# Attention pooling over 512 behaviour sequences: the fourth group of each chunk split into high and low halves, two of the four relus on ScalarE, a four-column maximum step, and natural tiles loaded two chunks behind the transposed ones

## What is computed

```python
W_b, W_c = (fc1_w[:E], fc1_w[E:])
h = relu(einsum('bse,eh->bsh', behavior_emb, W_b) + (candidate_emb @ W_c)[:, None, :] + fc1_b)
scores = einsum('bsh,h->bs', h, fc2_w[:, 0]) + fc2_b[0]
attn = softmax(scores, axis=-1)
user_interest = einsum('bse,bs->be', behavior_emb, attn)
x = concatenate([user_interest, candidate_emb], axis=1)
z = relu(x @ mlp1_w + mlp1_b)
logit = (z @ mlp2_w + mlp2_b)[:, 0]
```

## Time and profile before

| | |
|---|---|
| median of 3 runs | 282.52 us (282.26 to 283.63) |
| profiled execution, its own time | 283.16 us |
| its span | 281.4 us |
| PE / PEld / DVE busy | 96% / 68% / 86% of the span |
| ACT / POOL busy | 54% / 10% |
| HBM read | 105.70 MB |
| mean granted TensorE clock | 0.987 of full speed |

### The profile page before, as it was taken

How to read it: one execution, slowest core, us unless ns; L and a number is a source line. 1 busy time by engine, 2 the same in 40 slices (tenths; PEclk the granted TensorE clock), 3 DMA queues, 4 the chain that set the end, 5 groups by cost and what they waited for, 6 DMA issues and landing times.

```text
span 281.4 us, 8325 instructions
## 1 busy us (share of the span) xinstructions
PE 269.7 (96%) x2934; PEld 190.7 (68%) x2934; DVE 241.9 (86%) x405; ACT 152.1 (54%) x397; POOL 28.8 (10%) x38
## 2 busy tenths in 40 slices
PE   5987998999999999999999999999999999999896
PEld 5655665767766776767766776767766776767563
DVE  1598879999999999999999999999999999999451
ACT  4365536665555556665555556665555556664312
POOL 2001101111111011111111011111111011111100
PEclk9599999999999999999999999999999999999999
DMA  7999999999999999999999999999999999970000
GB/s 236 436 428 427 423 417 430 425 420 428 429 420 431 426 424 431 424 424 433 422 426 431 424 426 429 426 424 428 428 426 428 422 429 428 424 306 0 2 3 0
DMA packets 10505, 105.83 MB, mean 376 GB/s; under 512 B 1152, under 2 KB 1664, under 8 KB 2432
## 3 DMA queue, kind: packets, MB, share of 16 engines
q1 hardware_dynamic: 10352, 105.39, 89.1%
q10 hardware_dynamic: 144, 0.31, 0.4%
HBM read 105.70 MB, written 0.00 MB: 376 GB/s over the span
## 4 chain that ended last, share of the span: by engine, by line
PE 83%; DMA 11%; issue 2%; DVE 1%; SPq 1%; ACT 1%; DVEq 0%; ACTq 0%
PE s_ps L583 15%; PE u_ps L593 15%; PE z_ps L562 14%; PE z_ps L566 13%; PE z_ps L570 11%; PE z_ps L567 11%; DMA xt<-in_behavior_t 11%; PE z_ps L593 1%; SPq L224 1%; ACT xh L296 1%; PE u_ps L621 1%; PE z_ps L662 1%; PE z_ps L656 1%; PE z_ps L642 0%; DVE hidden L428 0%
## 5 line engine op out<-in xcount | busy, mean ns | idle before, releaser
L428 DVE TENSOR_TENSOR hidden<-z_ps,neg_bias 128x800 f32<-128x800 f32 x96 | 94.5, 988 | 9.7 <-PE z_ps L570 6.3
L418 DVE TENSOR_TENSOR xl<-xt,xh 128x800 fp32r<-128x800 f32 x96 | 94.7, 987 | 4.7 <-ACT xh L296 4.7
L296 ACT CAST xh<-xt 128x800 fp32r<-128x800 f32 x96 | 81.0, 860 | 13.1 <-DMA xt<-in_behavior_t 11.7
L566 PE MATMUL z_ps<-xh,w_hi 128*128 128x512 f32 x192 | 75.6, 394 | 2.9 <-DVE hidden L428 2.9
L567 PE MATMUL z_ps<-xh,w_lo 128*128 128x512 f32 x192 | 63.9, 348 | 0.0
L593 PEld LDWEIGHTS u_ps<-x,weights_by_row 128*32 128x32 f32 x1500 | 46.5, 110 | 12.3 <-issue 12.3
L570 PE MATMUL z_ps<-xl,w_hi 128*128 128x512 f32 x192 | 51.3, 349 | 0.0
L583 PE MATMUL s_ps<-hidden,f_col 128*1 128x384 f32 (+1 forms) x512 | 49.6, 505 | 1.6 <-issue 1.4
L265 POOL TENSOR_TENSOR weights_by_row<-weights,first_sb 128x400 f32<-128x400 f32 x31 | 26.9, 869 | 235.6 <-ACT weights L306 235.6
L593 PE MATMUL u_ps<-x,weights_by_row 128*32 128x128 f32 x1500 | 50.8, 273 | 0.0
L562 PE MATMUL z_ps<-xt,first_sb 128*128 128x288 f32 (+1 forms) x128 | 48.3, 500 | 0.0
(11 more groups left out here) (71 smaller groups left out, 100.9 us busy)
## 6 DMA issues: line engine op xcount, KB each, us to landing
x<-in_behavior SPq DMA_DIRECT2D x32, 1600.0 KB, 13.9
xt<-in_behavior_t SPq DMA_DIRECT2D x31, 1600.0 KB, 15.3
xt<-in_behavior_t SPq DMA_DIRECT2D x4, 400.0 KB, 5.4
first_sb<-in_first ACTq DMA_DIRECT2D x1, 307.5 KB, 4.5
later_sb<-in_later SPq DMA_DIRECT2D x1, 258.5 KB, 19.2
cand<-in_candidate SPq DMA_DIRECT2D x1, 192.0 KB, 5.3
cand<-in_candidate SPq DMA_DIRECT2D x1, 64.0 KB, 4.4
out_logit<-logit SPq DMA_DIRECT2D x1, 1.8 KB
```

Source lines behind the costliest of these rows:

```text
L296: nc.scalar.copy(xh[g][:, :], xt[q][:, g, :]).then_inc(xh_made, 1)
L418: nc.vector.tensor_tensor(xl[g][:, :], xt[q][:, g, :], xh[g][:, :].bitcast(F32), ALU.subtract).then_inc(xl_made, 1)
L428: nc.vector.tensor_tensor(hidden[q % 2][:, g, :, :].rearrange("p t (b s) -> p t b s", s=PARTS), z, nb.to_broadcast([P, TILES, EACH, PARTS] ...
L566: nc.tensor.matmul(z[:, a:b], w_hi[:, :], xh[g][:, a:b], start=True, stop=False)
```

## The change

Four parts. (1) Group 3 is split like the others: `xh` and `xl` get a fourth buffer, and the float32 product of L562 goes. (2) ScalarE takes the relu of groups 1 and 3, VectorE the maximum of groups 0 and 2. The order of both engines' lists changes with it, and in the round of chunk 0 ScalarE makes both relus ahead of all four high halves of chunk 1. (3) Step 3 of the softmax writes 4 columns in place of 32, and step 4 transposes a broadcast view of them. (4) SP loads the natural tile of c-2, not of c-1, behind the transposed one of c; the latter waits for `xl` of (c-4, 3), not for the products.

```diff
-SPLIT = GROUPS - 1
+HALF = GROUPS // 2
...
-        xh = [sb(f"xh{i}", [P, WIDTH], F32R) for i in range(SPLIT)]
-        xl = [sb(f"xl{i}", [P, WIDTH], F32R) for i in range(SPLIT)]
+        xh = [sb(f"xh{i}", [P, WIDTH], F32R) for i in range(GROUPS)]
+        xl = [sb(f"xl{i}", [P, WIDTH], F32R) for i in range(GROUPS)]
...
-            for c in range(1, XT_BUFS):
-                sp.dma_start(xt[c][:, :, :], behavior_t[c, :, :, :]).then_inc(xt_loaded[c], 16)
-                sp.dma_start(x[c - 1][:, :], behavior_v[c - 1, :, :]).then_inc(x_loaded[c - 1], 16)
-                if c == 2:
-                    sp.dma_start(later_sb[:, :], later).then_inc(later_loaded, 16)
-            with sp.Fori(0, CHUNKS // X_BUFS - 1) as turn:
+            def load_transposed(c, buf):
+                if buf is None:
+                    buf = c
+                else:
+                    sp.wait_ge(xl_made, (c + (1 - XT_BUFS)) * GROUPS)
+                sp.dma_start(xt[buf][:, :, :], behavior_t[c, :, :, :]).then_inc(xt_loaded[buf], 16)
+            def load(c, buf):
+                if buf is None:
+                    buf = c
+                else:
+                    sp.wait_ge(pooled_done, c + (1 - X_BUFS))
+                sp.dma_start(x[buf][:, :], behavior_v[c, :, :]).then_inc(x_loaded[buf], 16)
+            load_transposed(1, None)
+            for c in range(2, X_BUFS):
+                load_transposed(c, None)
+                load(c - 2, None)
+            sp.dma_start(later_sb[:, :], later).then_inc(later_loaded, 16)
+            for c in range(X_BUFS, 2 * X_BUFS):
+                load_transposed(c, c - X_BUFS)
+                load(c - 2, None if c - 2 < X_BUFS else c - 2 - X_BUFS)
+            with sp.Fori(0, CHUNKS // X_BUFS - 2) as turn:
                 for j in range(X_BUFS):
-                    c = turn * X_BUFS + (X_BUFS + j)
-                    before = (j + X_BUFS - 1) % X_BUFS
-                    sp.wait_ge(z_done, (c + (1 - XT_BUFS)) * GROUPS)
-                    sp.dma_start(xt[j][:, :, :], behavior_t[c, :, :, :]).then_inc(xt_loaded[j], 16)
-                    sp.wait_ge(pooled_done, c - X_BUFS)
-                    sp.dma_start(x[before][:, :], behavior_v[c - 1, :, :]).then_inc(x_loaded[before], 16)
-            sp.wait_ge(pooled_done, CHUNKS - X_BUFS)
-            sp.dma_start(x[X_BUFS - 1][:, :], behavior_v[LAST, :, :]).then_inc(x_loaded[X_BUFS - 1], 16)
+                    c = turn * X_BUFS + (2 * X_BUFS + j)
+                    load_transposed(c, j)
+                    load(c - 2, (j + 2) % X_BUFS)
+            load(LAST - 1, X_BUFS - 2)
+            load(LAST, X_BUFS - 1)
...
-            def biased_relu(c, q, phase):
-                act.wait_ge(z_done, c * GROUPS + GROUPS)
-                if phase <= 1:
+            def biased_relu(c, q, g, phase):
+                act.wait_ge(z_done, c * GROUPS + (g + 1))
+                if phase <= 1 and g == 1:
                     act.wait_ge(bias_made, 1 + phase)
-                if phase >= 2:
+                if phase >= 2 and g == 1:
                     act.wait_ge(scores_done, c - 1)
-                z = z_view(q, GROUPS - 1)[:, 0:WIDTH].rearrange("p (t r) -> p t r", r=Q)
+                z = z_view(q, g)[:, 0:WIDTH].rearrange("p (t r) -> p t r", r=Q)
                 for b in range(EACH):
                     mine = slice(b * PARTS, (b + 1) * PARTS)
-                    op = nc.scalar.activation(hidden[q % 2][:, GROUPS - 1, :, mine], z[:, :, mine], ACT.Relu,
-                                              bias=bias[:, bass.ds(c * ROWS + (GROUPS - 1) * EACH + b, 1)])
+                    op = nc.scalar.activation(hidden[q % 2][:, g, :, mine], z[:, :, mine], ACT.Relu,
+                                              bias=bias[:, bass.ds(c * ROWS + g * EACH + b, 1)])
                 op.then_inc(relu_made, 1)
...
             copy_candidates(1)
+            high_half(0, 0, 3, (xt_loaded[0], 16), True)
...
+                if phase == 0:
+                    positive_bias(0)
+                    biased_relu(c, q, 1, phase)
+                    bias_times_f2()
+                    positive_bias(1)
+                    biased_relu(c, q, 3, phase)
+                    for g in range(GROUPS):
+                        next_half(g)
+                    return
                 flush = phase >= 2 and (q - 2) % 2 == 1
                 next_half(0)
+                biased_relu(c, q, 1, phase)
                 next_half(1)
-                if phase == 0:
-                    positive_bias(0)
-                    bias_times_f2()
-                    positive_bias(1)
                 if flush:
                     copy_pooled4(c - 2, u_ps)
-                if phase >= 1:
-                    exponents(c - 1, (q + 1) % 2, phase <= 2)
+                exponents(c - 1, (q + 1) % 2, phase <= 2)
                 next_half(2)
-                biased_relu(c, q, phase)
+                biased_relu(c, q, 3, phase)
                 if flush:
                     copy_pooled_t(c - 2, u_ps)
+                next_half(3)
...
                 if step == 3:
-                    each = part_max_t[:, :].rearrange("p (b s) -> p b s", s=PARTS).unsqueeze(2)
-                    op = nc.vector.tensor_reduce(row_max_wide[:, :].rearrange("p (b s) -> p b s", s=PARTS),
-                                                 each.to_broadcast([P, EACH, PARTS, PARTS]), axis=AX.X, op=ALU.max)
+                    op = nc.vector.tensor_reduce(row_max_t[:, :],
+                                                 part_max_t[:, :].rearrange("p (b s) -> p b s", s=PARTS),
+                                                 axis=AX.X, op=ALU.max)
                 if step == 4:
-                    op = nc.vector.transpose(row_max[:, :], row_max_wide[:, :])
+                    op = nc.vector.transpose(row_max[:, :].rearrange("p (b s) -> p b s", s=PARTS),
+                                             row_max_t[:, :].unsqueeze(2).to_broadcast([P, EACH, PARTS]))
...
                 biased_max(c, q, 0, phase < 2)
-                biased_max(c, q, 1, phase < 2)
+                low_half(c, q, 3)
...
-                if g % GROUPS == SPLIT:
-                    pe.wait_ge(relu_made, c + (g // GROUPS + 1))
-                else:
-                    pe.wait_ge(hidden_made, c * SPLIT + (g // GROUPS * SPLIT + g % GROUPS + 1))
+                pe.wait_ge(relu_made if g % 2 else hidden_made, c * HALF + (g // 2 + 1))
             def products(c, q, g, early):
                 z = z_view(q, g)
                 halves = [(0, BANK), (BANK, WIDTH)]
-                if g < SPLIT:
-                    pe.wait_ge(xh_made, c * SPLIT + (g + 1))
-                else:
-                    pe.wait_ge(xt_loaded[q], loads(c, q))
+                pe.wait_ge(xh_made, c * GROUPS + (g + 1))
                 if not early:
                     banks_read(c, g - Z_BACK[q * GROUPS + g])
-                if g == SPLIT:
-                    for a, b in halves:
-                        op = nc.tensor.matmul(z[:, a:b], w_b, xt[q][:, g, a:b], start=True, stop=True)
-                    op.then_inc(z_done, 1)
...
-                pe.wait_ge(hidden_made, c * SPLIT + SPLIT)
-                pe.wait_ge(relu_made, c + 1)
+                pe.wait_ge(hidden_made, c * HALF + HALF)
+                pe.wait_ge(relu_made, c * HALF + HALF)
...
-            row_mask & (p % PARTS == 0), (p < SPLIT * Q) & (p % Q // PARTS == np.arange(EACH)[None, :]),
+            row_mask & (p % PARTS == 0), (p // Q % 2 == 0) & (p % Q // PARTS == np.arange(EACH)[None, :]),
...
```

More of the change, by code:

```diff
@@ L84, in attention_pooling_kernel @@
         part_max_t = sb("part_max_t", [P, Q])
-        row_max_wide = sb("row_max_wide", [P, Q])
+        row_max_t = sb("row_max_t", [P, EACH])
         row_max = sb("row_max", [P, Q])
@@ L415, in low_half @@
             def low_half(c, q, g):
-                dve.wait_ge(xh_made, c * SPLIT + (g + 1))
+                dve.wait_ge(xh_made, c * GROUPS + (g + 1))
                 nc.vector.tensor_tensor(xl[g][:, :], xt[q][:, g, :], xh[g][:, :].bitcast(F32),
@@ L553, in products @@
                 halves = [(0, BANK), (BANK, WIDTH)]
-                if g < SPLIT:
-                    pe.wait_ge(xh_made, c * SPLIT + (g + 1))
-                else:
-                    pe.wait_ge(xt_loaded[q], loads(c, q))
+                pe.wait_ge(xh_made, c * GROUPS + (g + 1))
                 if not early:
                     banks_read(c, g - Z_BACK[q * GROUPS + g])
-                if g == SPLIT:
-                    for a, b in halves:
-                        op = nc.tensor.matmul(z[:, a:b], w_b, xt[q][:, g, a:b], start=True, stop=True)
-                    op.then_inc(z_done, 1)
-                    return
                 for a, b in halves:
@@ L567, in products @@
                     nc.tensor.matmul(z[:, a:b], w_lo[:, :], xh[g][:, a:b], start=False, stop=False)
-                pe.wait_ge(xl_made, c * SPLIT + (g + 1))
+                pe.wait_ge(xl_made, c * GROUPS + (g + 1))
```

(4 more changed lines are left out.)

## The result

The changed kernel takes 279.49 us (median of 4 runs, 278.73 to 280.04), the kernel before 282.62 beside it: ratio 0.9882 [0.9846, 0.9918], faster by 1.2%. Run again on another chip it took 277.91 (5 runs, 276.98 to 278.08) beside 283.05, ratio 0.9821 [0.9807, 0.9834]. The forecast was 277.8, in a range of 273.5 to 281.8: 4.9 us less, where the first pair of medians gives 3.1 less and the second 5.1. The first profiled execution took 279.17 us with a span of 277.4, 4.0 less than the one before.

The account below looks back on a forecast made before the run. Loads bound the start up to chunk 3's scores, TensorE's work the 27 rounds after. Terms: 1.3 - 6.1 and 0.1 less at the end, -4.9 on 283.16, thus 278.3; median forecast 277.8 us, range 273.5 to 281.8.

Parts of the forecast that it names:

- The rounds: 27 rounds after the scores of chunk 3: splitting group 3 saves TensorE 0.225 us each, 7.69 a round, 6.1 us less.
- VectorE and ScalarE keep up: Within a round of 7.69 us: VectorE needs 7.25 (7.45 at worst) and ScalarE 6.43, so TensorE stays the bound.
- Rival (c): In the rounds: ScalarE becomes the bound at 8.0 us; 3.7 us more, 286.2 us; chance 0.09.
- The start: Up to the scores of chunk 3: relus ahead of chunk 1's high halves move them from 46.01 to 47.3, 1.3 us more.
- The list behind the relu of (0, 1): In the start: chunk 1's first high half at 18.85, done 19.7; then VectorE's 10.75 us of work, to 30.5.
- The sign for being wrong: Forecast is wrong if scores of chunk 3 start before 45, or rounds differ from 7.69 by over 0.1.
- rival (b): Rounds save only 3.4 us, and the start loses some 0.7 to TensorE's half-speed clock; 281.0 us; chance 0.22.
- Loads: In the start: the new order lands transposed tiles 3.84 us earlier, but VectorE's list covers this, worth nothing.
- rival (a): In the start: VectorE isn't held, loads set the scores of chunk 3 at 42.1; 272.4 us; chance 0.13 with halfway cases.
- Step 3 and the end: Softmax's third step on VectorE takes 0.2 us less than 0.42; last chunk's group 3 saves 0.1 us.

Follow-up runs that it names:

- Experiment 5: Changed kernel with group 3 unsplit again (one float32 product, no halves), all else as in the change; 286.12 us, ratio 1.0113.
- Experiment 10: Changed kernel with the softmax's third step as before (128 x 256 elements into 128 x 32) and a plain transpose after it; 278.33 us, ratio 0.9847.
- experiment 6: Changed kernel with the maximum of group 1 left on VectorE, all four groups split; 293.36 us, ratio 1.0373.
- Experiment 9: Changed kernel run a second time, unaltered; 277.91 us, ratio 0.9821.
- experiment 1: Changed kernel with ScalarE making chunk 1's high halves among the biases and relus of chunk 0's round, not behind both relus; 274.39 us, ratio 0.9727.
- experiment 7: Changed kernel with ten warm-up matmuls in place of seven, run twice; 277.65 us (ratio 0.981), then 276.92 us (ratio 0.979).
- experiment 2: Changed kernel with the old order of loads, natural tile of c-1 behind the transposed one of c; 278.68 us, ratio 0.9858.
- experiment 3: Kernel before with the new order of loads alone, its transposed tiles still waiting for the products; 281.40 us, ratio 0.9955.
- experiment 4: Kernel of experiment 1 with the old order of loads, natural tile of c-1 behind the transposed one of c; 276.29 us, ratio 0.976.

## Why the prediction was right, and where it was not

**The rounds: right, in mechanism and size.** 7.69 was forecast, 7.68 measured; 1.10 for the group behind group 3, as said; -6.2 for -6.1 in 27 rounds. Experiment 5 shows the cause: without the split the round is 7.92, a difference of 0.24 for the 0.225 of the sum. Of the 0.20 that I chose between 0.10 and 0.25 for the round with the transposition, 8.02 - 7.81 = 0.21 came.

**VectorE and ScalarE keep up: right.** Experiment 10 tried the 7.45 that was the worst of the forecast for VectorE, with 38.18 of 40 us busy there for 36.84, and the round stayed. With 0.90 more (experiment 6) the round is 8.13, for 8.15 worked out from the same rows. That is also the measurement for the rule of the Trainium skill that relu belongs on VectorE ("ScalarE: Activation LUTs", "Rules for kernel authors"): the operation is cheaper there, and this kernel is slower for it, 293.36 us against 277.91 to 279.49, since VectorE is the fuller engine. Rival (c) did not come: ScalarE is busy 33.45 of 40 us, 6.42 in a round of 7.68, for 6.43 in the sum.

**The start: the mechanism right, the size off, and it is not one size.** The list behind the relu of (0, 1) was right: 5.95 us to the first low half of chunk 1 for 6.18 forecast. The step that was off was "That of (0, 1) can start when TensorE's result is there, 13.57", taken from the earlier trace rows, which is one execution's moment. In that execution TensorE was granted 0.50 from 8 to 14 us and took 0.63 us for 512 columns; there the loads bound the start. By first and second profile of the changed kernel:

| | forecast | first | second |
|---|---|---|---|
| relu of (0, 1) | 13.57 | 14.73 | 11.84 |
| first low half of chunk 1 | 19.75 | 20.68 | 17.80 |
| scores of 1 | 31.9 | 33.06 | 30.89 |
| scores of 3 | 47.3 | 48.44 | 46.26 |
| against 46.01 | +1.3 | +2.4 | +0.2 |
| profiled execution | 278.3 | 279.17 | 276.98 |

The forecast lies in the middle by luck: the term is +1.3 with 1.1 to either side. Experiment 9 excludes a fixed extra cost; experiment 1 shows that the whole term hangs on ScalarE's order, since the same instructions in another order take the scores of 3 to 43.77. The sign for being wrong, scores of 3 ahead of 45, did not come.

The moment itself goes with TensorE's speed ahead of it. Six profiled executions have this order of the start (split group 3, relu of (0, 1) on ScalarE, high halves last):

| | products from 7 us up to the relu | relu of (0, 1) | first low half | scores of 3 |
|---|---|---|---|---|
| first profile | half speed | 14.73 | 20.68 | 48.44 |
| experiment 10 | full, then half from 8.2 to 14.8 | 13.95 | 19.91 | 48.75 |
| experiment 7, first | half, full from 11 | 13.17 | 19.15 | 47.78 |
| experiment 2 | half, full from 10.7 | 12.77 | 18.73 | 47.41 |
| second profile | full speed | 11.84 | 17.80 | 46.26 |
| experiment 7, second | full speed | 11.76 | 17.72 | 46.21 |

The longer TensorE ran at half speed, the later the relu; the low half follows it by 5.95 to 5.98 in all six. The scores of 3 in experiment 10 stand later than that alone would give: VectorE waited 0.99 us for the scores of chunk 0 there (below), and its step 3 is the long one. The last two and experiment 10 ran on one chip. Something under 0.5 us of the spread can come from the first constants, for which ScalarE waits: its first conversion of the weights starts between 5.29 and 5.76. This is read from traces: no experiment set the speed, and experiment 7, which was to do it, didn't.

**The clock of rival (b) came in, and its price depended on the rest.** The first profile's windows:
```profile
17.00:20.00 3.00, 1.49 (x14) 0.94 (x6) 0.00 (x0) 1.61 (x6) 0.00 (x0) 1.00 1.03 439
20.00:26.00 6.00, 4.74 (x16) 3.39 (x20) 5.25 (x9) 3.79 (x5) 0.00 (x0) 0.50 1.00 425
26.00:27.00 1.00, 1.00 (x8) 0.24 (x12) 1.00 (x3) 1.00 (x4) 0.00 (x0) 0.59 0.97 410
```
After the thinly filled stretch the clock is granted at 0.50, that is 1.2 GHz, up to 26 us and over. In the first profile VectorE's list hid it: 33.06 - 20.68 = 12.4 from the first low half to the scores of 1, for 12.15 forecast. In the second it is 30.89 - 17.80 = 13.1. VectorE's transposition of the scores of chunk 0 shows why, in the first and in the second profile:
```profile
27.95 0.62 DVE L461 STREAM_TRANSPOSE scores<-s_ps 128x416 f32<-128x416 f32 x1
...
25.77 0.62 DVE L461 STREAM_TRANSPOSE scores<-s_ps 128x416 f32<-128x416 f32 x1 [0.78 <-PE s_ps L594]
```
TensorE made these scores in 1.98 us in the first, since the clock rose within them, and in 2.68 in the second; VectorE waited 0.78 for them there, and 0.99 in experiment 10. So the 0.7 us that the rival gave were paid by the second execution, and not by the first.

**Loads: right that they are worth nothing here, wrong about what stands behind them.** Experiment 2 confirms the first. But "by loads alone they could start at 42.1" was the floor of rival (a), and no kernel reached it: 44.48 in experiment 3, 43.77 in experiment 1. The engines' own lists are the next bound, 1.5 us behind the loads in the kernel before. No order tried here reached rival (a)'s 272.4; whether another could is open.

**Step 3 and the end: right.** 0.23 for some 0.2, covered; behind the scores of 30 the change saves 0.2 us for the 0.1 of the sum.

## What to carry to other kernels

Where the order of an engine's list is written out, look at the prologue's list on its own: here it kept some 4 of the 8 us that the change could give, and the high halves at other places of ScalarE's list made 274.4 us of 277.9 to 279.5, the best version of this study. When an engine has a cheaper instruction for an operation, ask which engine is fuller before moving it there. And when a change takes the cover off a stretch, take the spread of that stretch into the range: a moment read from one execution is a sample, not a constant.

## What the runs showed of the hardware that was not expected

**TensorE's speed in the start.** The first profile's windows view grants 1.00 from 7 to 20 us, here a part of it:
```profile
10.00:14.00 4.00, 3.43 (x10) 2.23 (x9) 2.86 (x4) 1.45 (x3) 0.00 (x0) 1.00 1.01 429
14.00:17.00 3.00, 2.92 (x17) 2.03 (x15) 0.00 (x0) 2.27 (x6) 0.00 (x0) 1.00 0.99 422
```
The products there say otherwise; two of 512 columns in a row, PE's timeline:
```profile
14.49 0.63 PE L577 MATMUL z_ps<-xh,w_hi 128*128 128x512 f32 x1
14.91 0.63 PE L578 MATMUL z_ps<-xh,w_lo 128*128 128x512 f32 x1
```
They start 0.42 us apart; in the rounds it is 39.60 - 39.37 = 0.23. The second profile of the same kernel, in the products of (0, 0) and at the same place in the program:
```profile
7.21 0.40 PE L578 MATMUL z_ps<-xh,w_lo 128*128 128x512 f32 x1
...
11.64 0.39 PE L577 MATMUL z_ps<-xh,w_hi 128*128 128x512 f32 x1
11.88 0.40 PE L578 MATMUL z_ps<-xh,w_lo 128*128 128x512 f32 x1
```
In experiment 10 the record gives 0.50 at such products (13.71 and 14.13, both 0.63 us). So early in a trace, ahead of the first change that it records, the granted clock can say 1.00 while the products run at half speed, and their distance is the better reading. The moment at which they got fast differed between executions of kernels with the same start: about 16.5 us in the first profile, 15 in experiment 10 (after a fall at 8.2), 10 to 11 in experiment 2 and in the first profile of experiment 7; in the second profile and in the second of experiment 7 they were fast from 7 us on. What decides it is open.

**The spread.** With its start bound by TensorE's results a kernel varies: the changed kernel 278.73 to 280.04 on one chip and 276.98 to 278.08 on another, experiment 2 276.89 to 279.94 on one. With the start bound by loads it varied less in experiment 4 (276.15 to 276.38), but the kernel before, bound by loads too, spread by 1.0 to 2.2 us beside each set of experiments (282.15 to 283.22, 282.61 to 284.82, 282.42 to 283.38). So this is a tendency in few runs.
